# The first self attention of a decoder: heads in quarters of the array, four batches per projection

## The reference, cut to what matters

```python
x = x + _L0_attn_ref(_layernorm(x), W_Q, b_Q, W_K, b_K, W_V, b_V, W_O, b_O)
# inside, all float32:
Q = einsum('btd,hkd->bthk', x, W_Q) + b_Q        # K and V likewise
attn = softmax(einsum('bqhk,bshk->bhqs', Q, K) / sqrt(64))
out_h = einsum('bhqs,bshk->bqhk', attn, V)
out = einsum('bqhk,hdk->bqd', out_h, W_O) + b_O
```

## Time and profile before

| | us |
|---|---|
| median of 3 runs | 4392.98 (4380.46 to 4395.82) |
| profiled execution, its span | 4385.31, 4383.5 |
| busy in the span: PE, DVE, ACT, POOL | 3747.9, 2630.2, 2132.7, 1548.2 |
| first and last instruction of this stage's attention (first product, last addition) | 38.97, 293.11 |

### The profile page before, as it was taken

The page is one execution under the profiler, slowest core; times in us unless marked ns, Lnnn a source line. Parts: engine busy times, 40 slices in busy tenths (PEclk is TensorE's granted clock), DMA queues, the critical chain, the costliest instruction groups (busy, mean ns, idle before and its releaser), DMA issues. The chain is left out here.

```text
span 4383.5 us, 107819 instructions
## 1 busy us (share of the span) xinstructions
PE 3747.9 (85%) x45374; PEld 2609.8 (60%) x45374; DVE 2630.2 (60%) x4484; ACT 2132.7 (49%) x2865; POOL 1548.2 (35%) x1827
## 2 busy tenths in 40 slices
PE   6988638999998796779999996988889999984598
PEld 5866315777776345647777774433457777762476
DVE  5643357877775454548777773335578777755643
ACT  2233445766665233337666663344456666652010
POOL 0000007666763000046676660003376666630000
PEclk9989769999999799989999998998999999995698
DMA  3008016555563230045566650100165555630475
GB/s 141 0 22 319 2 25 159 147 148 148 146 150 76 69 97 18 0 115 145 143 151 152 154 137 29 53 33 8 27 154 147 144 149 146 154 77 1 114 191 145
DMA packets 203340, 464.36 MB, mean 106 GB/s; under 512 B 87630, under 2 KB 94543, under 8 KB 202607
## 3 DMA queue, kind: packets, MB, share of 16 engines
q1 hardware_dynamic: 201486, 457.86, 40.3%
q10 hardware_dynamic: 1440, 0.52, 0.1%
HBM read 213.51 MB, written 1.72 MB: 49 GB/s over the span
## 5 line engine op out<-in xcount | busy, mean ns | idle before, releaser
L1333 DVE TENSOR_REDUCE x_bank_top<-ps 112x1 f32<-112x500 f32 x2304 | 1418.7, 671 | 515.6 <-PE ps L1074 508.9
L1201 ACT ACTIVATE x_probs_t<-ps 128x1344 f32<-128x1344 f32 x768 | 991.1, 1291 | 214.6 <-PE ps L1091 210.2
L1091 PEld LDWEIGHTS ps<-x_queries,x_keys 128*128 128x128 bf16 x9216 | 487.4, 98 | 334.2 <-issue 153.0
L1074 PE MATMUL ps<-x_keys,x_queries 96*112 96x500 bf16 x2304 | 632.3, 380 | 5.9 <-DVE x_bank_top L1333 3.9
L1091 PE MATMUL ps<-x_queries,x_keys 128*128 128x112 bf16 x9216 | 584.7, 213 | 42.1 <-ACT x_probs_t L1201 36.6
L1104 PE MATMUL ps<-x_probs_t,x_values 128*32 128x112 f32 x18432 | 489.4, 262 | 4.1 <-ACT x_probs_t L1201 4.1
L1104 PEld LDWEIGHTS ps<-x_probs_t,x_values 128*32 128x32 f32 x18432 | 442.6, 111 | 68.6 <-issue 63.6
L1273 POOL TENSOR_TENSOR x_key_part<-x_key_whole,x_nothing 128x500 bf16<-128x500 f32 x279 | 347.9, 1247 | 273.2 <-ACT x_key_whole L1188 273.2
L1293 POOL MEMSET x_nothing<- 128x500 f32 x3 | 1.5, 514 | 1169.8 <-issue 1169.8
L1277 POOL TENSOR_TENSOR x_key_part<-x_key_left,x_nothing 128x500 bf16<-128x500 f32 x279 | 351.4, 1259 | 21.9
L1062 PE MATMUL ps<-x_wv,x_ctx_t 128*128 128x128 f32 (+1 forms) x2304 | 329.8, 287 | 2.7 <-ACT x_key_whole L1188 2.6
(11 more groups left out here) (447 smaller groups left out, 4805.0 us busy)
## 6 DMA issues: line engine op xcount, KB each, us to landing
x_keys<-x_key_part SPq DMA_DIRECT2D x1152, 192.0 KB, 3.7
x_ctx_t<-in_ctx_t SPq DMA_DIRECT2D x96, 750.0 KB, 6.0
cm_ctx_n<-in_ctx_n SPq DMA_DIRECT2D x32, 768.0 KB, 7.0
cm_ctx_t<-in_ctx_t SPq DMA_DIRECT2D x32, 750.0 KB, 9.0
e_share<-m_weight_scratch SPq DMA_DIRECT2D x32, 490.0 KB
e_spread_out<-m_slot_scratch SPq DMA_DIRECT2D x32, 490.0 KB
x_queries<-x_query_part SPq DMA_DIRECT2D x558, 28.0 KB, 2.6
e_share<-m_weight_rows SPq DMA_DIRECT2D x32, 448.0 KB, 5.7
```

Source lines behind the costliest of these rows:

```text
L1074: nc.tensor.matmul(ps[0:RW, n, 0:KB], queries[i // 2 % 2][0:TALL, p, i % 2, :], keys[i % 2][0:TALL, p, KB * n:KB * n + KB], start=True, st ...
L1091: mm = nc.tensor.matmul(ps[:, TURNED + c // VC, RW * (c % VC):RW * (c % VC) + RW], keys[i % 2][:, p, KT * c:KT * c + KT], queries[i // 2 % ...
L1201: nc.scalar.activation(probs_t[PROBS[p]].rearrange("k (n c) r -> k n (c r)", c=VC), ps[:, TURNED:TURNED + VR, 0:VC * RW], ACT.Exp, scale=s ...
L1333: nc.vector.tensor_reduce(bank_top[0:RW, p, n:n + 1], ps[0:RW, n, 0:KB], AX_X, ALU.max).then_inc(topped, 1)
```

## The change

`self_attention_0` is rewritten. *Projections* take four batches (a group g, 4 x 56 = 224 columns, read straight from xn), in eight tiles t of two products each, which use PSUM banks 0 and 1 in turn; ScalarE keeps the tiles with t % 4 of 0 and 1, VectorE those of 2 and 3, each in one SBUF tile for four batches. One half of the next group's tiles (queries or keys) is made in each step (`halves`). *Scores*: a product per head and batch over the 64 rows of its head, 56 x 56, its place in the 128 x 128 array being one of four quarters (row half: head parity, column half: batch); no block diagonal. *Mixing*: a product per head and batch, 64 stationary columns and 56 moving, again in a quarter. *Values* are kept in one copy. *Softmax*: the multiplication by the inverse goes to GpSimd, and the zeros of probs are set there. *Output product*: once for four batches (224 columns). The bias of V goes through W_O once (`sum_biases`) and is added with b_O. Everything is written out: no loop, no register. W_O and b_V are laid out anew on the host.

```diff
-            def project_qk(n, u):
...
+            def project(g, t):
+                wait(pe, kept_act if t % 4 > 1 else kept_dve, kept_before(g, t))
+                if t % 4 == 1:
+                    wait(pe, added, g - 2 + t // 4)
+                w = (wq, wk)[t // 4]
+                for half in range(2):
+                    j = 2 * (t % 4) + half
+                    mm = nc.tensor.matmul(ps[:, t % 2, GC * half:GC * half + GC], w[:, P * j:P * j + P], xn[:, GB * g:GB * g + GB, 0:S],
+                                          start=True, stop=True)
+                mm.then_inc(made, 1)
...
+            def make_scores(n):
...
+                wait(pe, shifted, n)
                 for j in range(HJ):
-                    for b in range(2):
-                        mm = nc.tensor.matmul(ps[64 * b:64 * b + 64, 4 * u + 2 + j // 4, P * (j % 4):P * (j % 4) + P],
-                                              q[u][:, j, SP * b:SP * b + SP], k[u][:, j, b].rearrange("p h s -> p (h s)"),
-                                              start=True, stop=True)
+                    for odd in range(2):
+                        for b in range(2):
+                            r, cols = slice(64 * odd, 64 * odd + 64), slice(S * (2 * (n % 2) + b), S * (2 * (n % 2) + b) + S)
+                            mm = nc.tensor.matmul(ps[64 * b:64 * b + S, SCORES + odd, S * j:S * j + S], q[g % 2][r, j, cols], k[g % 2][r, j, cols],
+                                                  start=True, stop=True)
                 mm.then_inc(scores_done, 1)
...
+            def mix_values(n):
+                pe.wait_ge(probs_kept, n + 1)
                 pe.wait_ge(v_kept, n + 1)
                 for j in range(HJ):
+                    for odd in range(2):
+                        for b in range(2):
+                            r, column = slice(64 * odd, 64 * odd + S), S * (2 * (j // 2) + b)
+                            mm = nc.tensor.matmul(ps[64 * (j % 2):64 * (j % 2) + 64, TURN + odd, column:column + S],
+                                                  v[n % 2][r, b, DH * j:DH * j + DH], probs_t[r, j, SP * b:SP * b + S], start=True, stop=True)
                 mm.then_inc(mixed, 1)
...
+            for t in range(TILES):
+                project(0, t)
+            sum_biases()
+            for n in range(-1, NP_):
+                if n >= 0:
+                    turn(n)
+                if n + 1 < NP_:
+                    make_scores(n + 1)
+                if n > 0 and n % 2 == 0:
+                    project_out(n // 2 - 1)
+                for g, t in halves(n):
+                    project(g, t)
+                if n >= 0:
+                    mix_values(n)
+                if n + 1 < NP_:
+                    make_values(n + 1)
+            project_out(GROUPS - 1)
...
         @block.scalar
...
+            for n in range(-1, NP_):
+                if n >= 0:
+                    keep_turned(n)
+                for g, t in halves(n):
+                    if t % 4 < 2:
+                        keep_made(g, t)
+                if n + 1 < NP_:
+                    exponentials(n + 1)
+                    keep_values(n + 1)
...
+        @block.gpsimd
...
+            for n in range(NP_):
+                pool.wait_ge(inverse_ready, n + 1)
+                nc.gpsimd.tensor_tensor(by_parity(n % 2), by_parity(n % 2), spread(inverse[:], 3, S), ALU.mult).then_inc(probs_ready, 1)
...
         @block.vector
...
+            for n in range(-1, NP_):
+                if n + 1 < NP_:
+                    shift(n + 1)
+                if n > 0 and n % 2 == 0:
+                    add(n // 2 - 1)
+                for g, t in halves(n):
+                    if t % 4 > 1:
+                        keep_made(g, t)
+                if n + 1 < NP_:
+                    add_up(n + 1)
+                if n >= 0:
+                    keep_mix(n)
+            add(GROUPS - 1)
```

More of the change, by code:

```diff
@@ L278, in self_attention_0, with by_parity, halves, place @@
         bq, bk, bv = (sbuf(n, [P, HJ]) for n in ("bq", "bk", "bv"))
[L279 to L287, removed]
+        bo, bo_sum = sbuf("bo", [P, 1]), sbuf("bo_sum", [P, 1])
+        q, k = ([sbuf("%s%d" % (n, u), [P, HJ, GC]) for u in range(2)] for n in "qk")
+        v = [sbuf("v%d" % u, [P, 2, HJ * DH]) for u in range(2)]
+        probs = [sbuf("probs%d" % u, [P, HJ, 2, SP]) for u in range(2)]
+        probs_t, mix = sbuf("probs_t", [P, HJ, P]), sbuf("mix", [P, HJ, GC])
+        top, total, inverse = (sbuf(n, [P, 2, HJ]) for n in ("top", "total", "inverse"))
+        scores = ps[:, SCORES:SCORES + 2, 0:CT].rearrange("p o (j s) -> p o j s", s=S)
+        def by_parity(u):
+            return probs[u].rearrange("p j o s -> p o j s")[:, :, :, 0:S]
+        def halves(n):
+            g, h = (n + 3) // 2, (n + 1) % 2
+            return [(g, t) for t in range(4 * h, 4 * h + 4)] if 0 < g < GROUPS else []
+        def place(t):
+            whole, bias = ((q, bq), (k, bk))[t // 4]
+            return whole, bias, 2 * (t % 4)
+        def kept_before(g, t):
+            return 4 * g + 2 * (t // 4) + t % 4 - 1
+        def wait(engine, semaphore, value):
+            if value > 0:
+                engine.wait_ge(semaphore, value)
         block = own.enter_context(nc.Block(no_gpsimd_drain=True))
@@ L400, in _, with keep_made @@
-            act.wait_ge(pads_clear, 1)
-            take_tokens(0, 0)
-            all_pairs(act, one_step)
+            def keep_made(g, t):
+                whole, bias, first = place(t)
+                act.wait_ge(made, TILES * g + t + 1)
+                wait(act, scores_done, 2 * (g - 1))
+                for half in range(2):
+                    j = first + half
+                    last = nc.scalar.activation(whole[g % 2][:, j, :], ps[:, t % 2, GC * half:GC * half + GC], ACT.Identity, bias=bias[:, j:j + 1])
+                last.then_inc(kept_act, 1)
@@ new lines, in _ @@
+            act.wait_ge(landed, 8 * 16)
+            for t in range(TILES):
+                if t % 4 < 2:
+                    keep_made(0, t)
+            for n in range(-1, NP_):
+                if n >= 0:
+                    keep_turned(n)
+                for g, t in halves(n):
+                    if t % 4 < 2:
+                        keep_made(g, t)
[3 more added lines that the diff above has]
+        @block.gpsimd
@@ L458, in _, with keep_made @@
-            last.then_inc(pads_clear, 1)
-            dve.wait_ge(landed, 8 * 16)
-            all_pairs(dve, one_step)
+            def keep_made(g, t):
+                whole, bias, first = place(t)
+                dve.wait_ge(made, TILES * g + t + 1)
+                wait(dve, scores_done, 2 * (g - 1))
+                nc.vector.tensor_tensor(whole[g % 2][:, first:first + 2, :], ps[:, t % 2, 0:2 * GC].rearrange("p (h c) -> p h c", h=2),
+                                        spread(bias[:, first:first + 2], 2, GC), ALU.add).then_inc(kept_dve, 1)
```

201 lines of the change are left out of this document (83 added, 118 removed).

## The result

The changed kernel took 4322.5 us (median of 4 runs, 4317.2 to 4326.8), the kernel before 4390.5 (4 runs, 4380.5 to 4395.8): ratio 0.986, with a 95% interval of 0.984 to 0.988 (the quotient of the two medians, 0.985, lies inside it). In microseconds the medians moved by 68.0; the ratio and its interval stand for 61, from 53 to 69. Forecast were 4320 and a range of 4303 to 4354. The profiled execution of the changed kernel took 4326.8 us, with a span of 4325.1.

What follows compares the result with a forecast made beforehand. TensorE was taken as the bound; 16 + 6 x 22.0 + 9.45 + 27, with 4.7 for the clock, gave a stage of 189.2 us, ending 69.2 earlier: 4316, raised halfway to the median to 4320, range 4303 to 4354.

Steps and rivals of the forecast that it cites:

- Output product: TensorE's output product: 16 passes for two pairs, 3.12 us, or 1.56 a pair against 2.73 with its wait.
- Scores: TensorE's scores burst: 64 passes of 56 columns, all four quarters running together, 0.93 us.
- B: Rival on scores and mixing: row halves take turns, scores 1.67 and mixing 3.6 us, time 4351; chance 0.22.
- D: Rival on both bursts: changing the row half drains the array, scores 4.6, mixing 6.5 us, time 4443; chance 0.05.
- E: Rival on both bursts: nothing overlaps and nothing drains, scores 3.2, mixing 3.6 us, time 4376; chance 0.04.
- the floor: Rival on TensorE's issue: about 25 ns from start to start, scores 1.8 us, time 4334; chance 0.03.
- Mixing: TensorE's mixing burst: 64 passes, each product running beside one neighbour, 1.9 us.
- Queries and keys: TensorE's projections: 32 passes of 0.195 us for two pairs, 6.24, or 3.12 a pair against 3.64.
- The chain: Softmax from scores through GpSimd's product to transposes at 8.5 us: step 9.45, 0.5 of it waiting, two pairs 22.0.
- Rival C: Rival on the softmax chain: GpSimd's product takes 3.0 us instead of 1.9, 1.1 more per step, time 4338; chance 0.14.
- The move costs some 0.45 a step, 7 us: Division moved to GpSimd: 1.9 us in place of VectorE's 1.09 on the chain, a loss over the stage.
- Start and end: Stage's ends: first product at 34.7, 16 us to first transposes, last three steps 27; half clock adds 1.7 and 3.

Runs made afterwards that it cites:

- row_halves_apart: Changed kernel with all scores and mixing products of one row half of the array issued before those of the other; 4346.0 us, ratio 0.993.
- mixing_between_tiles: Changed kernel with mixing, quarters alternating, between the second and third projection tile, and VectorE's sum, reciprocal and mixing copy ahead of both its tiles; 4307.2 us, ratio 0.983.
- div_on_vector: Changed kernel with the softmax multiplication by the inverse moved from GpSimd back to VectorE, behind the reciprocal; 4337.8 us, ratio 0.990.
- changed_again: The changed kernel itself, unaltered, run again in a later set beside the kernel before; 4312.5 us, ratio 0.985.

## Why the prediction came out right, step by step

*The bound and its extent.* Right: TensorE bounded the stage, and the stage's end moved by 68.7 us where 69.2 were summed up. That the medians of four runs each moved by 68.0 as well is partly luck: the recorded ratio stands for 53 to 69, and the two profiled executions moved by only 58.5 (4385.3 to 4326.8), because what stands behind this stage differed by 10 us between them. That the forecast of 4320 and the measured 4322.5 are so close is luck too: it stands on the profiled execution's 4316 and a step halfway back to the median that no row supports; the sum put on the median whole gives 4393.0 - 69.2 = 4323.8.

*Output product* 3.12, measured 3.13: a 224-column pass takes 0.196. *Scores* 0.93, measured 0.97: the assumption that no row of before could show, four quarters at work together, holds. Rivals B (1.67), D (4.6), E (3.2) and the floor (1.8) fall on this number, and row_halves_apart shows what B looks like. The Trainium skill ("TensorE: Matmul & The Clock Gate", Back-to-back issue gap) has some 25 ns from start to start. The trace does not agree: 64 passes in 0.97 us are 15 ns each.

*Mixing* was mis-sized: 1.9, measured 1.21. The step that failed is "each product runs beside one neighbour". That is what mixing costs with one row half at a time (1.91 in row_halves_apart); with both it comes near the 1.03 of all four quarters together. Two products in a row on a quarter cost nearly nothing against a strict alternation (1.21 and 1.08), and eight in a row cost all (3.31). The price of a product alone on its quarter, 0.107, was about right: eight in a row cost 0.103 each (3.31 / 32). What was wrong is how much of it the other quarters hide. How long a run on one quarter may be before it costs lies between two and eight products, and no run says where.

*Queries and keys* were mis-sized the other way: 3.32 with the wait, measured 3.61 to 3.63, no less than the 3.64 of before. The products are 3.0 of it; the rest is the third tile's wait for ScalarE and, behind each halt, a weight load that nothing covers. mixing_between_tiles gives 0.19 of it back. The gain forecast on this line, 0.3 a pair, did not exist; that of the output product did (2.73 to 1.57 a pair, its wait for x included).

*The chain.* The product on GpSimd 1.9, measured 1.69; the sum at 5.0 behind the start of scores, measured 5.25 when the output product's 3.13 is taken off (124.72 - 116.34 - 3.13); the transposes at 8.5, measured 8.44. So the step of 9.45 came out to the hundredth, and that is luck: the sum started 0.25 late and the product on GpSimd was 0.21 short, and the two cancel. Rival C, which had 3.0 for that product, falls on the 1.69. The wait is 0.69 where 0.5 was forecast: the chain decides, so the errors in mixing (-0.7) and tiles (+0.3) only turned into waiting. TensorE's own step is 8.76, where 9.0 were forecast. The Trainium skill ("GPSIMD Engine Reference", 4.1 Engine selection) makes GpSimd about twice as slow with two inputs; 1.69 against 1.09 for the same product is 1.55.

*"The move costs some 0.45 a step, 7 us"* is the wrong statement of the prediction. It priced the multiplication on the chain, but not VectorE's copy of mixing, which the transposes need too and which would stand behind it. div_on_vector shows the opposite sign: the move gains 0.42 a step.

*Start and end.* The first product came at 32.8 instead of 34.7, since the weights were issued 1.8 us earlier; the norm ahead had ended earlier, which I had held fixed. This is chance, not the change (eight passes of the norm took 4.73 to 6.14 us in the seven profiles looked at, the longest in the kernel before), and it took back what the stage ran over: 191.6 us instead of 189.2. The overrun is nearly all in the start: 19.57 to the first transposes where 16 + 1.7 were booked; the thirteen steps took 141.7 for 141.45, and what follows the transposes at 194.04 took 30.4 for 27 + 3. The start's first 16 passes at the 1.2 GHz level took 5.7 us, and behind the wait of 3.22 before 202.60 the clock was low (0.50 from there to 206.19): four bursts there and at the end took 1.97, 1.76, 4.53 and 4.96 instead of 1.09, 1.05, 3.29 and 3.29, which is 4.5 us where 3 were booked. Before the last of them TensorE had stood for only 1.10 and 1.18 us. What these waits do differs from run to run: in changed_again the same 1.10 and 1.18 left the last burst at 3.29, and in row_halves_apart TensorE stood for 2.99 before its transposes at 217.67, which then took the 1.09 of full clock.

*Where the 3.8 us a pair came from* (14.81 to 11.02): mixing by head 2.49, output product 1.16, scores 0.92, projections 0, transposes and the new wait -0.8. Of the parts of the change, the early start gave 6 us of stage (4 without the earlier norm), mixing head by head 27, as shown alone in the old loop on two quarters, and keeping row halves interleaved 0.67 a step, 8.6 over the thirteen steady steps (the last additions lie 14 apart, 237.71 against 223.96, but that run also had a clock of 0.76 from 44 to 60 us). Writing the loop out was not tried by itself.

## What to carry to other kernels

Block diagonals and half-empty operands cost time on TensorE's array: mixing took 3.70 us with 32 passes of 128 stationary columns and 1.21 with 64 smaller ones. Heads of 64 features fit a quarter, and if the order goes round all four quarters with at most two products in a row on each, some two thirds of their time is hidden (3.31 us alone, 1.21 and 1.08 so); if it stays in one row half, less (1.91). When an operation is moved to a slower engine, count what stood behind it on the faster one and who waits for that, not its length alone. Once a burst is cut below its softmax chain, only what stands on that chain counts: here one tile moved behind a sum was worth 0.75 us a step, and a mixing burst shorter by 0.13 nothing.

## What was not expected of the hardware

Stages far behind the change, with unchanged code, differ from execution to execution with the granted clock. Rows of one window each: the stage of the experts near the end, in the changed kernel, with the early sum and alternating quarters, and with the division on VectorE:

```profile
4032.50:4315.40 282.90, 256.33 (x1295) 192.36 (x1296) 116.31 (x99) 27.64 (x55) 0.00 (x0) 0.88 0.66 169
```
```profile
4007.90:4278.20 270.30, 242.26 (x1296) 183.91 (x1296) 116.11 (x99) 27.63 (x55) 0.00 (x0) 0.93 0.69 177
```
```profile
4042.00:4332.10 290.10, 260.01 (x1295) 195.87 (x1296) 116.47 (x99) 27.63 (x55) 0.00 (x0) 0.87 0.66 165
```

The same 1296 passes take 242 to 260 us of TensorE as the clock goes from 0.93 to 0.87; the 99 instructions of VectorE do not change. And the first rotary attention, in the kernel before and in the same kernel with the early start:

```profile
2950.50:3054.80 104.30, 93.62 (x1280) 42.88 (x1280) 62.73 (x90) 44.03 (x128) 31.94 (x32) 0.89 0.01 2
```
```profile
2948.80:3062.00 113.20, 101.28 (x1280) 46.92 (x1280) 63.09 (x90) 44.57 (x127) 32.08 (x32) 0.82 0.01 2
```

So a stage mark that repeats to 0.01 us can stand beside a total that moves by 10 us either way. Whether the moment at which a stage is reached sets its clock is only argued; no run isolates it.
